# An attention-and-experts layer on one core: first queries moved by groups of heads, routing fields written by GpSimd, halved low parts, a new order of attention's items

## The reference, cut to what matters

```python
# x (2, 1024, 256); 16 heads of 16, 4 key/value heads; 16 experts, the best 4 per token, one shared expert
q, k, v = x @ wq.T + bq, x @ wk.T + bk, x @ wv.T + bv
att = softmax(where(causal, rope(q) @ rope(k).T / 4, -inf))
x = layernorm(x + (att @ v) @ cp.T + cp_b)
scores = sigmoid(x @ gate_w.T) + gate_b
weights, indices = top_k(scores, 4); weights = weights / weights.sum(-1)
shared = (silu(x @ w1s) * (x @ w3s)) @ w2s
routed = sum over the 4: weight * (silu((x @ w1[e]) * (x @ w3[e])) @ w2[e])
out = layernorm(x + shared + routed)
```

## Time and profile before

| | us |
|---|---|
| median of 3 runs (535.23 to 536.46) | 535.52 |
| the profiled execution | 534.25 |
| its span, first to last instruction | 532.5 |
| PE, DVE, ACT, POOL busy in it | 506.3, 435.0, 373.2, 292.0 |

### The profile page before, as it was taken

The page is one execution under the profiler, slowest core; times in us unless marked ns, Lnnn a source line. Parts: engine busy times, 40 slices in busy tenths (PEclk is TensorE's granted clock), DMA queues, the critical chain, the costliest instruction groups (busy, mean ns, idle before and its releaser), DMA issues.

```text
span 532.5 us, 12191 instructions
## 1 busy us (share of the span) xinstructions
PE 506.3 (95%) x3775; PEld 359.0 (67%) x3775; DVE 435.0 (82%) x1102; ACT 373.2 (70%) x845; POOL 292.0 (55%) x340
## 2 busy tenths in 40 slices
PE   8789999999999999899999997999999999999895
PEld 5545554545454646355432696899999999999884
DVE  3699998899999999989971479978878877877685
ACT  3527878788988978769889573466766766667444
POOL 5404354454315677777778592777555445445292
PEclk9989999999999999999999999999999999999998
DMA  5464350074034893201422631577543433331595
GB/s 154 94 164 62 78 86 19 3 160 84 1 95 121 182 215 94 82 33 50 130 77 81 183 92 41 181 244 232 154 135 129 121 119 114 117 115 45 192 414 186
DMA packets 53182, 64.96 MB, mean 122 GB/s; under 512 B 8139, under 2 KB 46686, under 8 KB 53120
## 3 DMA queue, kind: packets, MB, share of 16 engines
q1 hardware_dynamic: 45072, 45.60, 32.0%
q0 software_dynamic: 7344, 18.38, 10.1%
q10 hardware_dynamic: 704, 0.20, 0.2%
HBM read 32.49 MB, written 25.62 MB: 109 GB/s over the span
## 4 chain that ended last, share of the span: by engine, by line
PE 63%; DVE 22%; ACT 6%; POOL 5%; issue 3%; DMA 1%; DVEq 0%; ACTq 0%; POOLq 0%
PE psH L1820 15%; DVE MX L1265 10%; PE psO L1602 8%; PE psS L1617 8%; PE psT L1587 7%; PE psX L1788 3%; PE psG L1831 3%; PE psS L1684 2%; ACT prob L953 2%; PE psY L1844 2%; PE psY L1848 2%; PE psY L1845 2%; PE psY L1847 2%; PE psY L1846 2%; PE psS L1622 2%
## 5 line engine op out<-in xcount | busy, mean ns | idle before, releaser
L953 ACT ACTIVATE prob<-psT 128x512 f32<-128x512 f32 (+3 forms) x384 | 166.0, 497 | 34.1 <-PE psT L1587 31.3
L1265 DVE TENSOR_REDUCE MX<-psS 128x1 f32<-128x512 f32 (+3 forms) x304 | 178.9, 652 | 5.0 <-PE psS L1622 2.0
L1617 PE MATMUL psS<-KS,QS 96*128 96x512 bf16 (+3 forms) x384 | 108.0, 330 | 5.2 <-DVE MX L1265 2.8
L906 POOL DMA_INDIRECT y_scratch<-ys,dst x79 | 77.0, 974 | 65.6 <-ACT ys L1115 50.6
L1587 PE MATMUL psT<-QS,KS 98*128 98x512 bf16 (+3 forms) x384 | 107.2, 328 | 0.4
L829 POOL DMA_INDIRECT xs_scratch<-x1row,slotu x64 | 64.8, 1012 | 30.4 <-issue 15.3
L1820 PE MATMUL psH<-wU,xh 128*128 (+1 forms) x380 | 80.9, 334 | 0.5 <-DVE z L1424 0.4
L1602 PE MATMUL psO<-prob,V 128*32 128x512 f32 (+3 forms) x768 | 75.9, 499 | 1.8 <-POOL prob L862 1.7
L862 POOL TENSOR_SCALAR_AFFINE_SELECT prob<-prob 128x512 f32<-128x512 f32 x64 | 42.2, 664 | 58.8 <-ACT prob L953 58.3
L1587 PEld LDWEIGHTS psT<-QS,KS 98*128 98x128 bf16 x384 | 34.5, 97 | 48.5 <-ACT prob L953 21.1
L1820 PEld LDWEIGHTS psH<-wU,xh 128*128 128x128 f32 x380 | 61.8, 189 | 1.2 <-issue 1.1
(11 more groups left out here) (278 smaller groups left out, 1004.0 us busy)
## 6 DMA issues: line engine op xcount, KB each, us to landing
xs<-xs_scratch SPq DMA_DIRECT2D x80, 134.0 KB
y<-y_scratch SPq DMA_DIRECT2D x16, 512.0 KB, 9.7
wU_raw<-in_L_ffn_w_routed_dram SPq DMA_DIRECT2D x32, 176.0 KB, 3.2
QS<-qp SPq DMA_DIRECT2D x42, 128.0 KB, 4.3
xs_scratch<-padrow SPq DMA_DIRECT2D x4, 536.0 KB
xs_scratch<-padrow SPq DMA_DIRECT2D x16, 134.0 KB
x1row<-in_L_attn_x_dram SPq DMA_DIRECT2D x4, 512.0 KB, 6.8
out_dram<-x1row SPq DMA_DIRECT2D x7, 256.0 KB, 2.9
```

The lines of the kernel that those rows point to most:

```text
L906: nc.gpsimd.indirect_dma_start(y4_dram, bass.IndirectOffsetOnAxis(ap=dst[:, n % NSEL, t:t + 1], axis=0), ys[:, n % NYS, t, :], None, bound ...
L953: nc.scalar.activation(prob[:, step % NPROB, h, 0:HALF - c0], ps[:, 0:HALF - c0], ACT.Exp).then_inc(s_Tfree, 1)
L1265: found = nc.vector.tensor_reduce(out=MX[:, c0 // HALF, heads[0]:heads[-1] + 1, i - TH * q], in_=src, op=ALU.max, axis=AX_X)
L1617: last = mm(ps[:, e * dist:e * dist + cols], QS[0:ROWS, QAT[(k // 2) % NSLOT], g % 2 * G + h, (i - TH * q) * P:(i - TH * q + 1) * P], KS[b ...
```

## The change

- **First queries by groups.** Of each query block with m = 0 (s = 0, 2, 4, 6) the rows are now stored by group of four heads, and each of its six transfers becomes two of half the size, one per head group. For block 0 POOL issues the six of group 0 first and then the six of group 1, and PE waits for head group 0 only for its own six (`s_first_q[0]`). For s = 2, 4, 6 SP issues twelve and both groups wait for all of them. The turned rotation is read through a view; POOL copies it once (`rq_first`) for the bias.
- **Fields.** DVE no longer writes expert numbers and shares into the rows. It marks hits from `idx` directly, doubles the sum and takes the reciprocal; POOL writes both fields just before the half's first scatter, after waiting for `s_slot` and `s_share`, and waits for its own two writes (`s_field`).
- **Low parts in halves.** POOL makes each low part of an up-projection with two instructions of 128x352 in place of one of 128x704 (ten in attention, seven in the hand-over). In the hand-over the first of the seven now stands behind the first row block's scale and shift in place of the second's.
- **Warm-up.** `ones_b` is filled first, PE waits for that one alone, and makes 11 warm-up products in place of 9.
- **Order.** `ORDER` is another table. After the last maximum 43 exponentials and two weight casts of ACT are left, where 42 and one were; between the freeing of slot 0 (after head group 7) and the first product of head group 12 stand 17 exponentials and 9 maxima, where 12 and 11 stood.

```diff
-WARM = 9
+WARM = 11
...
-aaaaaapdlapappdpldppaaaaaaaaaadaaaaalamapaaplapadxxxaaaxpxxxavxlaxaaxaxxavmaxaadaxdxpxaaxxaxvmvxaxaxaxaxaaexaxxpxvvxaxaa
+aaaaaappadadpllpdppaadlaaaaaaadaapapmaaaapaaaapaxxaxalxaxpmvxxaxaxaxlaaxxavxxaxaaxxaapaxxxavmvaxaxxaaxaxeaaxxpdxavvxxaxa
...
-LOWS_AFTER = {1: LASTU[0:1], 2: LASTU[1:2], 3: LASTU[2:]}
+LOWS_AFTER = {0: LASTU[0:1], 2: LASTU[1:2], 3: LASTU[2:]}
...
+        def turned_q(m):
+            return rq[:, m, :] if m else rq[:, m, :].rearrange("p (d a h) -> p a d h", a=2, h=G)
+        def transfers(s):
+            return len(PAIRS) * (1 if HEADGROUPS[2 * s][2] else 2)
-        def queries_in(s):
+        def queries_in(s, group):
             if s == 0:
-                return s_first_q, 16 * len(PAIRS)
-            return s_qload[s % NSLOT], 16 * len(PAIRS) * (s // NSLOT + (s % NSLOT > 0))
+                return s_first_q[group], 16 * len(PAIRS)
+            return s_qload[s % NSLOT], 16 * sum(transfers(r) for r in range(s % NSLOT, s + 1, NSLOT) if r)
...
+                    if m:
+                        engine.dma_start(to, src).then_inc(queries_in(s, 0)[0], 16)
+                        continue
+                    for group in groups:
+                        engine.dma_start(to[:, group * G:(group + 1) * G, :],
+                                         src[group * KVW:(group + 1) * KVW, :]).then_inc(queries_in(s, group)[0], 16)
...
+            pool.wait_ge(s_wq, 16 * WLOADQ)
+            nc.gpsimd.tensor_copy(rq_first[:, :].rearrange("p (a d h) -> p a d h", a=2, h=G), turned_q(0)).then_inc(s_turned, 1)
...
                     pool.wait_ge(s_const, CONSTS)
+                    pool.wait_ge(s_share, h + 1)
+                    nc.gpsimd.tensor_copy(x1row[:, tiles, ID], idx[:, :, 0:TOPK]).then_inc(s_field, 1)
+                    nc.gpsimd.tensor_tensor(x1row[:, tiles, WT], top[:, :, 0:TOPK], trec[:, :, :].to_broadcast([P, TH, TOPK]),
+                                            ALU.mult).then_inc(s_field, 1)
+                    pool.wait_ge(s_field, 2 * h + 2)
...
-                        queries(pool, 0, part)
+                        queries(pool, 0, part, (0,))
+                    for part in range(3):
+                        queries(pool, 0, part, (1,))
...
-                    nc.gpsimd.tensor_tensor(lo, raw, hi.bitcast(F32), ALU.subtract).then_inc(s_wlo2, 1)
+                    for k in range(KC):
+                        nc.gpsimd.tensor_tensor(lo[:, k, :], raw[:, k, :], hi[:, k, :].bitcast(F32), ALU.subtract).then_inc(s_wlo2, 1)
...
                 link(nc.vector.tensor_reduce(out=tsum[:, :, 0], in_=top[:, :, 0:TOPK], op=ALU.add, axis=AX_X))
-                link(nc.vector.reciprocal(trec[:, :, :], tsum[:, :, :]))
-                nc.vector.scalar_tensor_tensor(out=x1row[:, tiles, WT], in0=top[:, :, 0:TOPK], scalar=0.5,
-                                               in1=trec[:, :, :].to_broadcast([P, TH, TOPK]), op0=ALU.mult, op1=ALU.mult)
+                link(nc.vector.tensor_scalar(tsum[:, :, 0], tsum[:, :, 0], 2.0, None, ALU.mult))
+                nc.vector.reciprocal(trec[:, :, :], tsum[:, :, :]).then_inc(s_share, 1)
...
+                    if h:
+                        dve.wait_ge(s_field, 2 * h)
...
-                    link(nc.vector.tensor_copy(x1row[:, tiles, ID], idx[:, :, 0:TOPK]))
...
-            pe.wait_ge(s_const, 6)
+            pe.wait_ge(s_const, 1)
```

79 lines of the change are left out of this document (45 added, 34 removed).

## The result

The changed kernel takes 529.9 us (median of 6 runs, 528.78 to 533.39) against 535.33 for the one before on the same chips (6 runs, 533.74 to 536.46): a ratio of 0.9923, 95% interval 0.9899 to 0.9948. That is 5.4 us less, where 3.8 were forecast (531.7, range 528.8 to 535.0). A second set of runs on another chip gave 529.48 against 534.03, 0.9912 (0.9884 to 0.9939).

The account below looks back on a forecast made before the run. DVE's maxima were taken to set attention's pace, ACT's exponentials leading after the last maximum. Terms -1.3 - 2.1 - 0.5 - 0.6 + 0.7 = -3.8 us took the median of 535.52 to 531.7, range 528.8 to 535.0.

Parts of the forecast that it names:

- The start: Before DVE's first maximum: queries no longer hold DVE, first maximum 2.1 us earlier, at 23.6; net -1.3 us.
- The moved remainder: At the start: one remainder moves behind the first group of maxima, 1.4 us earlier; done later all the same, 0.75.
- the second piece of `xTl`: At the start on DVE: the second xTl, at 15.38 before, can run some 0.7 us earlier.
- The block at 222: In attention: DVE's share instruction no longer meets POOL's low part; -1.50 + 0.3 - 0.91 = -2.1 us.
- new meetings: Charge for other DVE instructions meeting POOL's: 0.3 us, from 0 to 1.5.
- Routing on DVE: Per half of rows DVE loses two small instructions and gains one, 0.18 us less: -0.5 us in attention.
- Six further transfers per block: On SP's queue: they lie beside other work, nothing charged; for block 6 a slower rival was named.
- DVE's standing: Between DVE's maxima: 15.0 us before; effect of the other moved items put at 0, within ±1.5.
- The hand-over: After attention: halved low parts shorten the gating's wait, -0.4, one routing instruction less, -0.2; -0.6 us.
- what is late next: In the hand-over: ten halves end at 323.1, five ended at 322.4; the first routed pair, at 323.62, needs them all.
- The end of attention: After the last maximum: ACT has one exponential and one cast more, 1.4 us, half charged: +0.7 us (0 to 1.4).
- more than that: Rival: half clock from 34.18 to 37.59 kept away (0.7), DVE stands 1.5 less; 529.5 us, chance 0.18.

Follow-up runs that it names:

- the second profile: The changed kernel, unaltered, profiled again: 529.32 us in that execution, 529.48 us in the median of its runs.
- the first profile: The changed kernel's first profiled execution, nothing altered: 533.39 us, the longest of its six runs.
- the best version: The changed kernel with wA's third weight piece issued ahead of query block 4 and whole low parts in the hand-over alone: 526.45 us, 0.9846 of the kernel before.

## Why the prediction was right, and where not

**The start: right, and too small.** A gain of 2.1 at the first maximum was forecast, 0.75 of it given back. It is 3.17 in the second profile (25.71 to 22.54). The chain is as described: the middle part follows the high part, DVE's last remainder ends it, no transfer is waited for. The moved remainder gives 1.39, as reckoned. The term that was too small is the second piece of `xTl`: it ends at 14.68 instead of 16.07, which is 1.39 earlier, not 0.7 (1.21 with the new table alone). And 0.4 was left out: before, the first maximum stood 1.11 us behind the beginning of the last remainder, because PE still waited for the queries, and now 0.67. A part goes with the clock: with the full clock at 6.0 to 6.4 us the piece ends at 14.8 to 15.4, and the whole gain is 2.4 to 2.8 (first maximum at 22.95, 23.06, 23.30). Whether the warm-up, which I had put at nothing, moves that clock is not shown.

Group 0's sixth transfer left at 17.9 and had landed by 21.2, where 18.9 and 21.9 were forecast. What the split does is seen on block 0 itself (POOL's issues), the twelve halves of the changed kernel and then the six of the kernel with whole query transfers, which has the same order:

```profile
DMA to landing us min/median/max: 2.6/3.1/3.5
```

```profile
DMA to landing us min/median/max: 3.1/5.0/5.9
```

The last of the six whole ones landed at 23.96, the last of the twelve halves at 23.71. So the split brings the block as a whole hardly sooner; it lets the half that is needed first land first, 2.7 us before. The Trainium skill (SBUF — State Buffer, "Can I just issue two DMAs to hit both halves?") says that two transfers on half the partitions each run one after the other; for the pair these rows agree. A consumer that waits for the first one alone gains all the same.

**What I took for one sum is a product, at the start.** I added the parts. Neither the table alone (534.34) nor the edits alone (535.05) gain anything in the median, both together 5 us. The four profiles, in us:

| | first maximum | DVE's work to the last maximum | DVE standing |
|---|---|---|---|
| before | 25.71 | 235.52 | 14.64 |
| the table alone | 25.27 | 236.78 | 11.61 |
| the edits alone | 25.07 | 233.49 | 16.14 |
| both | 22.54 | 233.59 | 13.62 |

Alone, the table and the edits bring the first maximum forward by 0.4 and 0.6, together by 3.2. Of DVE's work the edits take off 2 to 3 us with either table; with the old one, 1.5 of it comes back as standing. The table's own gain is in the standing. Shown for the start: PE's waits for queries are 1.31 us before, 3.03 with the table alone (the chain is early, the transfers whole), 0.75 + 2.75 with the edits alone (the transfers short, the chain late), and none with both; where PE waits 2.7 us or more there (also with whole query transfers), it runs 6.8 us at half clock around or after it, though the kernel before with the new warm-up does so too (29.8 to 36.7) with a wait of 1.35. Undone one at a time from the changed kernel, warm-up, fields, split and low parts cost 2.5, 2.2, 0.6 and 0. That these come to 5.3, about the whole gain, proves nothing, since each was measured with the table in place, and the 2.5 is not clear of the clock.

**The block at 222: right in kind, too small.** 1.5 of block less 0.3 for new meetings and 0.91 of waiting were forecast. The share instruction no longer meets a low part, and no routing instruction of DVE in attention takes 0.1 us more than its median now; summed over all DVE instructions there that run over 0.1 us above their median, the excess fell from 2.79 to 0.57 us, 2.2 where I had 1.2. Another 0.75 before, at 219.0 and 219.6, was lost beside POOL's row sums (`x1row`, L856); I had priced only the longest block, and in the new order these are gone as well, with no new ones. The half clock at 225 is gone with it. So the gain in attention is owed to the moved fields and the new order; that halving the low parts has a share in it is not shown (see the whole low parts above). The Trainium skill (SBUF — State Buffer, "Who interferes with whom") says a blocked instruction waits for the whole of the other; the halves bear it out where they do meet DVE: the most that DVE lost at once to a half was 0.76 us (the second gating of the hand-over, 1.00 where it takes 0.25 unblocked), to a whole low part 1.50.

**Routing on DVE: right.** DVE's busy time between the maxima should be 235.52 (250.16 less 14.64 of standing) - 0.5 - 2.22 (the blocks, as measured) + 0.75 (the moved remainder) = 233.55; it is 233.59.

**Six further transfers per block: wrong.** I said that they lie beside other work and looked only at block 6, where the changed kernel has no wait (PE waits for no transfer between 18 and 275 us). At block 4 the weights stood behind them in SP's queue, and that cost 2.24 us of DVE's standing. I had weighed who waits for the transfers, and not what is queued behind them. Of ACT's 2.35 us some 1.3 come from one issue among the twelve that took 1.92 us instead of 0.59; four profiles with the wait have one of 1.6 to 2.2 there, while in that of the whole low parts it takes 0.60, ACT waits 0.89 and PE 0.69. What makes it long stays open.

**The hand-over: wrong sign.** -0.6 forecast, +0.41 measured. The gating gained 0.34 as reckoned, and the low parts ended where they should (316.94; 323.1 less the shift of 6.1 is 317.0). The step that failed is "what is late next": I let the first routed pair wait for the low parts themselves. It waited for a DVE instruction behind `prs`, caught by the last halves. With whole low parts the stretch is 43.37, 0.16 under before, about the 0.2 that I had for the routing instruction less; the halves, which should have given 0.4, cost 0.57.

**The end of attention: wrong.** +0.7 was charged, 0.00 measured; from the last maximum to the last exponential it is 19.31 us in both kernels. ACT stands for PE there (0.56, 0.68 and 0.28 us before), so there was room for a further short exponential. A share of 85% busy does not say that one more instruction comes out at the end.

**Half clock.** The rival "more than that" named the stretch from 34.18 to 37.59, and it is absent in both profiles of the changed kernel. Its sum, 529.5, is near the measured 529.9, but by other amounts: it did not have the late weights nor the hand-over's loss. I had said that I am wrong if the first maximum is not before 25; in the first profile it is not (25.41), which goes with the late clock of that execution.

**The total: near partly by luck.** Between the two profiles the items measured are, with the forecast in brackets: the start -3.17 + 0.75 (-1.3), DVE's blocks -2.2 (-1.2), routing -0.5 (-0.5), DVE's standing -1.0 (-0.9), the hand-over +0.4 (-0.6), the end of attention 0 (+0.7), the experts' part +0.5 (nothing). Errors of up to 1.1 us of either sign make -5.15 out of -3.8. The standing came out as forecast only because two things that I had put at nothing nearly cancel: the new table saves some 2.4 us of it (11.33 in the best version, where 14.64 less 0.91 was due), and the late weights cost 2.24.

## What to carry to other kernels

Edits on one chain (the order of the items, the size of the transfer, the engine that issues) should be priced together: the chain ends at its slowest link, and shortening two links may give what neither gives alone. When a queue gets more entries, ask for each thing queued behind them when it is needed, not only whether the entries themselves are in time. A blocked instruction costs what stands behind it on the path: shorter pieces on the other engine mean shorter blocks, but more of them and a later end. And look up in the trace which instruction stood beside a blocked one: in attention it was a low part once in the kernel before, and row sums, scatters and cuts the other times.

## What the runs showed of the hardware

- The time at which PE got its full clock differed between executions of like kernels: about 4 to 7 us in most profiles, 13.9 in one. In two others the clock fell back to half between 9 and 15 us. The first maximum moved from 22.5 to 25.4 us by it alone, 2.9 us, more than most of the edits.
- Within the first 40 us, five of the nine profiles with both the new table and the split show no half clock after 15 us; all five profiles without one of the two do show one, of 3.4 or 6.8 us. PE's waits for queries may thus be worth more than their own length; it is not shown, for the other four show one as well without such a wait. In three of these four the full clock had come at 6.0 to 6.4 us and the half clock at 26.5 to 26.9; in the five without it, at 3.9 to 5.7, or at 13.9.
- DVE was blocked beside POOL's low parts, row sums, diagonal cuts and scatters alike: a share instruction of 0.18 us took 1.68 beside a low part, 1.20 beside two cuts, and the expert numbers, 0.17 in the median, 0.43 beside a scatter.
- In the experts' part one pair took 4.56 to 4.64 us instead of 4.01 in three profiles, both of the changed kernel among them; that is the +0.52 of the table. ACT stood there until a transfer of expert rows had landed. No edit goes with it, and its cause stays open. In the second profile:

```profile
348.80 0.84 ACT L1159 ACTIVATE ys<-psY,sel 128x256 f32<-128x256 f32 x2 [1.27 <-DMA y_scratch<-ys,dst]
```
